# The reciprocal root of the heads' norms: three Newton steps on VectorE for one power on GpSimd

## The chip, the cores and the metric

One core of one Trainium2 chip runs the whole program. The metric is device time in microseconds (us), from the program's start to its end. In the profile, PE is TensorE (matmuls), PEld its weight loads, DVE VectorE, ACT ScalarE, POOL GpSimd and SP SyncE, which issues most transfers.

## The reference, cut to what matters

Eight batches of 256 rows by 128 features go through four layers. Each layer is attention with 16 heads of 8 features, added to `x` through a gate, and then a feed-forward part, added in the same way. The four attentions differ a little (the third, number 2, is causal), and so do the feed-forward parts. The change bears on the fourth attention alone, number 3. It scores each query by its mean cosine with all keys, and only the best fifth of the queries attend:

```python
def _L3_xattn_ref(queries, keys, values, Wq, bq, Wk, bk, Wv, bv, Wo, bo):
    ...
    q_norm = q / jnp.linalg.norm(q, axis=-1, keepdims=True)
    k_norm = k / jnp.linalg.norm(k, axis=-1, keepdims=True)
    scores_all = jnp.einsum('bhqd,bhkd->bhqk', q_norm, k_norm)
    mean_scores = scores_all.mean(axis=-1)
    u = max(1, L_q // TOP_FACTOR)
    _, top_idx = jax.lax.top_k(mean_scores, u)
    ...
```

So for each batch the reciprocal norms of 256 x 16 keys and of as many queries are needed: one array of 128 partitions by 32 numbers (2 row tiles x 16 heads) for the keys and one for the queries.

## The kernel before, in words

Each of the eight batches is a stream of steps (`stream_steps`), and up to four streams are under way at once, in four slots of buffers. One list, `SCHEDULE`, merges the streams into a single fixed order; it comes from a string of digits written out by hand (`TURNS_TAKEN`), one digit for the batch whose next step is taken. Every engine walks the same list and issues its own instructions of each step in that order, so each engine's order is fixed, and an instruction that waits holds back all that stand behind it on its engine. Eight PSUM banks are shared by all steps; the order in which they are taken is a second string of digits (`BANKS_TAKEN`). PE fills a bank only when the one who last read it has said so.

The engines speak through counting semaphores. `signals` tells how often each step raises which one, and a `Ledger` works out from it the value to wait for. Within DVE, an instruction that reads what an earlier one wrote waits for that one's end: `end(...)` raises `dve_step`, `wait_end(...)` waits for it.

The steps that matter here:

- `key_rows` (3 parts, for the keys, while layer 2 ends) and `query_rows` (5 parts, between the score tiles of layer 3) both call `rows_norms`. Part 0 adds the bias to the projected rows out of PSUM (L1169), part 1 squares them (L1174), part 2 sums the squares of each head into `ss`, 128x32 (`head_sums`, L1182). On POOL, part 2 of the same step waits for `rows_ready` and raises `ss` to the power -0.5, into `rn` (L666). It raises `rn_ready`.
- `key_unit` waits on DVE for `rn_ready` and multiplies the key rows by `rn` (L1317); PE then takes their mean (`key_mean`, L942), which ends in `kbar`.
- `query_rows` also multiplies the rows by `kbar` and sums by head into `dot` (parts 2 and 3, L1355 and L1182). Part 4 waits for `rn_ready` and multiplies `rn` by `dot` (L1363). PE turns the result (`query_means`, L965), and DVE chooses the best 51 queries of each head in 14 steps of eight at a time (`choose`, L1373 and L1375).
- `norm` has a power of its own on POOL (`rstd`, 128x2, L612) and then two instructions that norm the rows (`h`, L619). In a stream it follows `key_rows`.
- `maxima` reduces each tile of attention scores, two banks at a time, on DVE (`mx`, L1389). PE writes the tiles (L872), and once more the other way round for the attention itself (`attend`, L894), whose exponentials are ACT's (L759).
- The feed-forward part of layer 2 holds PE longest: nine experts with two runs of matmuls each (`hidden`, L1075, and `output`, L1084), of which DVE adds the results (L1261).

Of the kernel before, what the change touches and what calls it, by code (L numbers as in the profile page):

```python
# [7 lines left out]
U32 = mybir.dt.uint32  # L8
ALU = mybir.AluOpType
# [3 lines left out]
P = 128  # L13
BATCHES, ROWS, D = 8, 256, 128
HEADS, HD = 16, 8
LAYERS = 4
SLOTS = 4
RT = ROWS // P
# [36 lines left out]
TWO_ONES = 0x3F803F80  # L55
MAGIC = 1.5 * 2.0 ** 20
EXPONENT = 0x7F800000


R_BV, R_BO, R_BQ3, R_BK3, R_BF3, R_GB = 0, 4 * D, 8 * D, 9 * D, 10 * D, 11 * D  # L60
# [108 lines left out]
def signals(step, b, l, part):  # L169

    s = b % SLOTS
    return {
        "load_x": {},
        "setup": {},
        "load_weight3": {},
        "weight3": {"b_full": int((b, part) == (0, FP6_PARTS)), "b_read": int((b, part) == (0, FP6_PARTS))},
        "load_ctx": {},
        "keys": {"a_full": 1, "a_read": 1, "b_full": 1, "b_read": 1, f"hi_ready{s}": 1, f"k_split{s}": 2, f"k_moved{s}": 16 * TERMS},
        "key_rows": {"a_full": int(part == 0), "a_read": int(part == 0), "rows_ready": int(part == 2), "rn_ready": int(part == 2)},
        "key_unit": {"rows_ready": 1},  # L180
        "key_mean": {"a_full": 1, "a_read": 1},
        "stats": {"var_ready": part},
        "norm": {f"h_ready{s}": 1, "rstd_ready": int(l == 0 and b < SLOTS), "xb_ready": int(l == 2 * LAYERS - 1)},
        "turn": {"b_full": 1, "b_read": 1},
        "query": {"b_full": 1, "b_read": 1, f"hi_ready{s}": 1, f"q_split{s}": 2, f"q_moved{s}": 16 * TERMS},
        "query_rows": {"a_full": int(part == 0), "a_read": int(part == 0), "rows_ready": int(part in (2, 4)), "rn_ready": int(part == 2)},
        "query_means": {"b_full": 1, "b_read": 1},
        "choose": {"sel_ready": int(part == 2 * ROUNDS - 1)},
        "chosen": {"a_full": 1, "a_read": 1},
        "maxima": {"a_full": 2, "a_read": 1},  # L190
        "max_parts": {"m_parts_done": part, "xb_ready": int(part == 0)},
        "max_turn": {"b_full": 1, "b_read": 1, f"m_moved{s}": 16},
        "attend": {"b_full": 2, "b_read": 2, "causal_ready": int(l == CAUSAL)},
        "weigh": {"pv_done": 1, "c_read": int(part % 4 == 3)},
        "max_clear": {f"m_cleared{s}": 16},
        "heads": {"a_full": RT, "a_read": 1},
        "heads_turn": {"b_full": 1, "b_read": 1},
        "project": {"a_full": 1, "a_read": 1},
        "route0": {name: int(part == 0) for name in ("a_full", "a_read", "b_full", "b_read")},
        "gelu0": {"cubic_ready": int(part == 1), "tanh_ready": int(part == 1)},  # L200
        "blend0": {"x_done": int(part == 2)},
        "logits": {"a_full": int(part == 0), "a_read": int(part == 0), "gap_ready": int(part == 2), "gap_exp": int(part == 2)},
        "combine": {"comb_ready": int(part == COMBINED)},
        "comb_turn": {"b_full": 1, "b_read": 1},
        "out_bias": {"a_full": RT, "a_read": RT},
        "hidden": ({"a_full": 2, "a_read": 2, "tanh_ready": 2} if l == 1 else {"b_full": 2, "b_read": 2}),
        "output": ({} if (l, part) == (1, EXPERTS) else {"b_full": 1, "b_read": 1, f"out_added{s}": 1} if l == 1
                   else {"a_full": 1, "a_read": 1}),
        "quantise": {"fp6_scaled": int(part == 2), "fp6_divided": int(part == 3),
                     "fp6_rounded": int(part == FP6_PARTS - 2), "xd_ready": int(part == FP6_PARTS - 1)},  # L210
        "affine3": {"a_full": RT, "a_read": RT},
        "store": {},
    }[step]
# [114 lines left out]
def flamingo(nc, x, ctxT, attn_w, bias_cols, bias_rows, g_all, router0, block0, router1, fc1, fc2,  # L328
             gate_up, down, router2, w1, ws1, b1_cols, w2, ws2, b2_all, w3, ident_in, causal_qk,
             causal_kq, before_in, iota_in, out):  # L330
    with ExitStack() as ctx:
# [3 lines left out]
        def two(name, shape, dt=F32):  # L335

            return [sb(f"{name}{s}", shape, dt) for s in range(SLOTS)]
# [36 lines left out]
        mhalf = sb("mhalf", [P, RT * HEADS])  # L374
# [28 lines left out]
        ss = two("ss", [P, RT * HEADS])  # L403
        rn = two("rn", [P, RT * HEADS])
        dot = two("dot", [P, RT * HEADS])
        kbar = two("kbar", [P, D])
        work = two("work", [HEADS, SENT + ROWS])
        top8q = two("top8q", [HEADS, 8])
# [10 lines left out]
        work_rows = [[t[:, i, :].rearrange("p (t d) -> p t d", t=RT) for t in raw] for i in range(4)]  # L419
# [13 lines left out]
        sems = {name: sem(name) for name in SEMAPHORES}  # L433
# [154 lines left out]
        def _(pool):  # L588
# [6 lines left out]
            w = Walk()  # L595
            for w.i, (step, b, l, part) in enumerate(SCHEDULE):
                s = b % SLOTS
                if step in ("keys", "query"):

                    name, parts = ("k", k_parts) if step == "keys" else ("q", q_parts)  # L600
# [8 lines left out]
                if step == "norm":  # L609
# [5 lines left out]
                    else:  # L615
                        power.then_inc(sems["pool_step"], 1)
                        pool.wait_ge(sems["pool_step"], w.step())
                        for r in range(RT):
                            ins = nc.gpsimd.tensor_scalar(h[s][:, r, :], (x_in if l == 0 else xs)[s][:, r, :], mv[s][:, r, 0:1],  # L619
                                                          rstd[s][:, r:r + 1], ALU.subtract, ALU.mult)  # L620
# [15 lines left out]
                if step == "output" and l == 1 and part != EXPERTS:  # L636

                    n = min(part, EXPERTS)
# [13 lines left out]
                if step == "quantise" and part in (3, FP6_PARTS - 1):  # L652
# [6 lines left out]
                    else:  # L659
                        pool.wait_ge(sems["fp6_rounded"], w.at_step("fp6_rounded", 1, "quantise", b, l, FP6_PARTS - 2))  # L660
                        nc.gpsimd.tensor_tensor(blocks(h[s][:, :, :]), blocks(y), per_block(sc3[s][:, :], RT), ALU.mult)\
                            .then_inc(sems["xd_ready"], 1)
                if step in ("key_rows", "query_rows") and part == 2:

                    pool.wait_ge(sems["rows_ready"], w.at("rows_ready", 1))
                    nc.gpsimd.tensor_tensor(rn[s][:, :], ss[s][:, :], mhalf[:, :], ALU.pow)\  # L666
                        .then_inc(sems["rn_ready"], 1)


        @block.scalar  # L670
# [426 lines left out]
        def _(dve):  # L1097
# [43 lines left out]
            w = Walk()  # L1141
# [9 lines left out]
            def end(ins, *what):  # L1151

                ins.then_inc(sems["dve_step"], 1)
                ended[what] = w.step()

            def wait_end(*what):

                dve.wait_ge(sems["dve_step"], ended[what])
# [6 lines left out]
            def rows_norms(part, name, s, bias):  # L1165

                if part == 0:
                    dve.wait_ge(sems["a_full"], w.at("a_full", 1))
                    nc.vector.tensor_tensor(work_rows[0][s][:, :, :],  # L1169
                                            a_bank(w, 1)[:, 0:RT * D].rearrange("p (t d) -> p t d", t=RT),  # L1170
                                            bias, ALU.add).then_inc(sems["a_read"], 1)
                if part == 1:
                    dve.wait_ge(sems["a_read"], w.at_step("a_read", 1, name, b, l, 0))
                    end(nc.vector.tensor_tensor(work_rows[1][s][:, :, :], work_rows[0][s][:, :, :],  # L1174
                                                work_rows[0][s][:, :, :], ALU.mult), name, "squares", b)
                if part == 2:
                    wait_end(name, "squares", b)
                    head_sums(ss[s], work_rows[1][s]).then_inc(sems["rows_ready"], 1)

            def head_sums(dst, src):  # L1180

                return nc.vector.tensor_reduce(dst[:, :].rearrange("p (c h) -> p c h", h=PAIRS),  # L1182
                                               src[:, :, :].rearrange("p t d -> p (t d)")
                                               .rearrange("p (c d h) -> p c h d", d=HD, h=PAIRS), AX.X, ALU.add)
# [103 lines left out]
            for w.i, (step, b, l, part) in enumerate(SCHEDULE):  # L1288
                s = b % SLOTS
                if step == "setup" and b == 0 and part != 2:  # L1290
                    set_up(part)
                if step == "weight3" and b == 0 and part < FP6_PARTS:
# [4 lines left out]
                    ins = fp6(part, 0, 1, w3_sb.unsqueeze(1), work_rows[0][0][:, 0:1, :])  # L1297
# [24 lines left out]
                if step == "stats" and part == 0:  # L1322
# [4 lines left out]
                    for r in range(RT):  # L1327
                        ins = nc.vector.bn_stats(stats[s][:, r, :], (x_in if l == 0 else xs)[s][:, r, :])
# [12 lines left out]
                if step == "norm" and l == 0 and b < SLOTS:  # L1341

                    dve.wait_ge(sems["rstd_ready"], w.at("rstd_ready", 1))
                    for r in range(RT):
                        ins = nc.vector.tensor_scalar(h[s][:, r, :], x_in[s][:, r, :], mv[s][:, r, 0:1],
                                                      rstd[s][:, r:r + 1], ALU.subtract, ALU.mult)
# [38 lines left out]
                if step == "maxima":  # L1385
                    r, keys, hp0, n = MAX_TILES[l][part]
# [42 lines left out]
                if step == "affine3":  # L1429
                    n = 2 * LAYERS - 1  # L1430
# [6 lines left out]
                if step == "route0" and part == 0:  # L1437
# [9 lines left out]
                    for r in range(RT):  # L1447
                        wait_end("above", b, r)
                        ins = nc.vector.scalar_tensor_tensor(junk[:, r, :], a_bank(w, 1)[:, 0:ROWS], col[s][:, 0, r:r + 1],
                                                             before[:, r, :], ALU.is_equal, ALU.mult,  # L1450
                                                             accum_out=col[s][:, 2, r:r + 1])
# [9 lines left out]
                if step == "gelu0":  # L1461
# [8 lines left out]
                    if part == 2:  # L1470
                        wait_end("kept", b)
                        for r in range(RT):
                            ins = nc.vector.tensor_scalar(h[s][:, r, :], h[s][:, r, :], col[s][:, 5, r:r + 1], None, ALU.mult)
                        end(ins, "skipped", b)
                if step == "blend0":
# [4 lines left out]
                    if part == 1:  # L1480
                        wait_end("gelu", b)
                        wait_end("skipped", b)
                        for r in range(RT):
                            ins = nc.vector.scalar_tensor_tensor(h[s][:, r, :], ffo[s][:, r, :], col[s][:, 4, r:r + 1],
                                                                 h[s][:, r, :], ALU.mult, ALU.add)
# [35 lines left out]
                if step == "quantise" and part not in (3, FP6_PARTS - 1):  # L1521
# [6 lines left out]
                    ins = fp6(part, s, RT, h[s][:, :, :], h[s][:, :, :])  # L1528
# [72 lines left out]
```

## Time and profile before

| | |
|---|---|
| time, median of three runs | 946.31 us (942.61 to 951.45) |
| time of the profiled execution | 943.03 us |
| its span, first to last instruction | 941.3 us |
| PE busy | 884.7 us (94%) |
| DVE busy | 699.1 us (74%) |
| ACT busy | 638.8 us (68%) |
| POOL busy | 497.7 us (53%) |

The span is what the profile's rows cover; the time of the execution holds some 1.7 us around it. A busy share is a mean over stages with different limits. A row of the timeline gives start, duration, engine, line, operation, operands with their shapes, and in brackets how long the engine stood idle before it and whose signal ended that. Neighbours on one engine can overlap by a little where neither waits for the other.

### The profile page before, as it was taken

The page shows a single profiled execution, that of the slowest core. Times are in us where ns is not written, and L with a number is a line of the kernel's source. Part 1 is how long each engine was busy: PE and PEld are TensorE (multiplying, and loading weights), DVE is VectorE, ACT ScalarE, POOL GpSimd, SP SyncE. Part 2 cuts the span into 40 slices and gives each one's busy share as a digit, 9 for nine tenths or more (in the row PEclk, how much of TensorE's full clock was granted, in tenths as well). Part 3 has the DMA queues.
Part 4 walks back from the last instruction along what each step waited for, and adds up shares of the span by engine and source line. Part 5 has one row for each costly group of instructions (what it writes and reads, how often), then busy time and mean ns, then how long its engine had stood idle before and what let it go on. Part 6 is the DMA issues. An engine that isn't in the chain of part 4 may idle for free.

```text
span 941.3 us, 21994 instructions
## 1 busy us (share of the span) xinstructions
PE 884.7 (94%) x8025; PEld 605.6 (64%) x8025; DVE 699.1 (74%) x2142; ACT 638.8 (68%) x1460; POOL 497.7 (53%) x627
## 2 busy tenths in 40 slices
PE   7898899999999999999987999999999999999976
PEld 3344457855899987468543365756588987878533
DVE  7898988777543278986998999797735356666897
ACT  2687667767774545798775767767797448786851
POOL 6447555875961234655366365557672625533173
PEclk9999999999999999999999999999999999999999
DMA  5433332321100010002102021111110010000000
GB/s 152 113 95 98 80 103 51 82 53 37 28 23 24 15 38 3 20 25 59 40 21 74 21 70 32 30 43 30 35 39 2 18 35 1 20 19 18 21 3 24
DMA packets 67515, 39.89 MB, mean 42 GB/s; under 512 B 8263, under 2 KB 65376, under 8 KB 67408
## 3 DMA queue, kind: packets, MB, share of 16 engines
q1 hardware_dynamic: 62608, 30.44, 12.6%
q0 software_dynamic: 2208, 6.78, 2.6%
q10 hardware_dynamic: 2592, 1.26, 0.5%
q8 instruction: 65, 1.06, 0.5%
q14 instruction: 42, 0.34, 0.1%
HBM read 11.12 MB, written 1.05 MB: 13 GB/s over the span
## 4 chain that ended last, share of the span: by engine, by line
PE 59%; DVE 19%; POOL 9%; ACT 4%; issue 3%; DMA 3%; SPq 2%; POOLq 0%; DVEq 0%; ACTq 0%
PE banks L1084 12%; PE banks L1075 12%; DVE mx L1389 9%; PE banks L1044 6%; PE banks L908 6%; POOL h L619 4%; PE banks L1054 4%; PE banks L894 4%; PE banks L859 3%; PE banks L872 3%; POOL rn L666 2%; ACT probs L759 2%; PE banks L852 2%; PE banks L1015 2%; POOL rstd L612 2%
## 5 line engine op out<-in xcount | busy, mean ns | idle before, releaser
L1389 DVE TENSOR_REDUCE mx<-banks 128x4 f32<-128x1024 f32 (+1 forms) x240 | 282.9, 1214 | 23.9 <-PE banks L872 17.1
L759 ACT ACTIVATE probs<-banks 128x512 f32<-128x512 f32 (+1 forms) x512 | 258.7, 583 | 47.3 <-PE banks L894 44.8
L812 ACT ACTIVATE probs<-banks,b_sb 128x256 f32<-128x256 f32 x288 | 118.0, 474 | 73.1 <-PE banks L1075 71.5
L908 PE MATMUL banks<-probs,v_aug 128*9 128x256 f32 (+1 forms) x2048 | 146.9, 369 | 6.4 <-ACT probs L759 5.4
L1084 PE MATMUL banks<-w_sb,probs 128*128 128x128 f32 x1152 | 140.6, 277 | 0.2 <-ACT probs L759 0.2
L1084 PEld LDWEIGHTS banks<-w_sb,probs 128*128 128x128 f32 x1152 | 134.9, 192 | 5.6 <-issue 2.5
L1075 PE MATMUL banks<-hT,w_sb 128*128 128x256 f32 x576 | 137.4, 382 | 0.1
L612 POOL TENSOR_TENSOR rstd<-veps,mhalf 128x2 f32<-128x2 f32 x64 | 46.2, 723 | 159.6 <-DVE veps L1336 159.3
L666 POOL TENSOR_TENSOR rn<-ss,mhalf 128x32 f32<-128x32 f32 x16 | 88.0, 5501 | 52.0 <-DVE ss L1182 51.6
L1075 PEld LDWEIGHTS banks<-hT,w_sb 128*128 128x128 f32 x576 | 104.5, 190 | 14.7 <-DVE xs L1261 0.8
L1261 DVE SCALAR_TENSOR_TENSOR xs<-banks,comb,xs 128x128 f32<-128x128 f32 x144 | 43.6, 343 | 86.6 <-PE banks L1084 86.4
L894 PE MATMUL banks<-q_st,k_st 64*128 64x256 bf16 (+1 forms) x1024 | 93.2, 268 | 4.9 <-DMA q_st<-mT 3.3
L872 PE MATMUL banks<-k_st,q_st 64*128 64x256 bf16 (+1 forms) x1024 | 88.9, 267 | 9.0 <-DVE mx L1389 4.8
L619 POOL TENSOR_SCALAR h<-xs,mv,rstd 128x128 f32<-128x128 f32 x112 | 90.8, 817 | 5.9
L644 POOL TENSOR_TENSOR xs<-xs,raw 128x256 f32<-128x256 f32 x72 | 52.8, 734 | 48.7 <-ACT raw L800 46.6
L894 PEld LDWEIGHTS banks<-q_st,k_st 64*128 64x128 bf16 x1024 | 34.5, 94 | 68.0 <-issue 23.0
L1044 PE MATMUL banks<-hT,fc_sb 128*128 128x256 f32 x320 | 77.0, 384 | 0.0
L690 ACT ACTIVATE hT<-banks 128x256 f32<-128x256 f32 x96 | 37.0, 390 | 58.1 <-PE banks L852 57.7
L908 PEld LDWEIGHTS banks<-probs,v_aug 128*9 128x9 f32 x2048 | 34.2, 88 | 60.7 <-ACT probs L759 24.7
L872 PEld LDWEIGHTS banks<-k_st,q_st 64*128 64x128 bf16 x1024 | 36.8, 94 | 55.3 <-issue 19.5
L650 POOL TENSOR_SCALAR_AFFINE_SELECT probs<-probs 128x512 f32<-128x512 f32 x64 | 40.6, 644 | 53.4 <-ACT probs L759 53.2
L1044 PEld LDWEIGHTS banks<-hT,fc_sb 128*128 128x128 f32 x320 | 57.8, 190 | 8.2 <-issue 0.6
(197 smaller groups left out, 1463.8 us busy)
## 6 DMA issues: line engine op xcount, KB each, us to landing
k_st<-k_parts SPq DMA_DIRECT2D x192, 64.0 KB, 2.1
q_st<-q_parts SPq DMA_DIRECT2D x186, 64.0 KB, 2.1
w_sb<-in_w POOLq DMA_DIRECT2D x16, 256.0 KB, 3.6
fc_sb<-in_fc POOLq DMA_DIRECT2D x6, 256.0 KB, 4.2
x_in<-in_x SPq DMA_DIRECT2D x8, 128.0 KB, 4.0
cT<-in_ctxT SPq DMA_DIRECT2D x8, 128.0 KB, 2.7
out_x<-xs SPq DMA_DIRECT2D x8, 128.0 KB, 1.9
q_st<-mT SPq DMA_DIRECT2D x32, 16.0 KB
```

The source lines that it names most:

```text
L612: power = nc.gpsimd.tensor_tensor(rstd[s][:, :], veps[s][:, :], mhalf[:, 0:RT], ALU.pow)
L619: ins = nc.gpsimd.tensor_scalar(h[s][:, r, :], (x_in if l == 0 else xs)[s][:, r, :], mv[s][:, r, 0:1], rstd[s][:, r:r + 1], ALU.subtract, ...
L666: nc.gpsimd.tensor_tensor(rn[s][:, :], ss[s][:, :], mhalf[:, :], ALU.pow)\
L759: nc.scalar.activation(probs[s][:, part % UNIT_RING, 2 * a:2 * a + 2, 0:n], b_bank(w, a + 1)[:, 0:2 * n].rearrange("p (j q) -> p j q", j=2 ...
L812: ins = nc.scalar.activation(hid[s][:, part % UNIT_RING, c, :], b_bank(w, half + 1)[:, j * ROWS:(j + 1) * ROWS], ACT.Gelu, bias=b1_sb[:, p ...
L872: ins = nc.tensor.matmul(a_bank(w, a + 1)[:, i * keys:(i + 1) * keys], head_rows(q_st, s, a, hp0 + i, r * P, P), head_rows(k_st, s, a, hp0 ...
L894: ins = nc.tensor.matmul(b_bank(w, a + 1)[:, j * n:(j + 1) * n], head_rows(k_st, s, a, 2 * g + j, t * P, P), head_rows(q_st, s, a, 2 * g + ...
L908: ins = nc.tensor.matmul(c_bank(b, l, u // 4)[VW * i:VW * i + VR, g % 2, q0:ROWS], v_aug[s][:, t, 4 * g + i, :], probs[s][:, u % UNIT_RING ...
L1044: ins = nc.tensor.matmul(a_bank(w, k + 1)[:, a * ROWS:(a + 1) * ROWS], fc1_sb[:, 2 * part + k, a, :], hT[s][:, :], start=True, stop=True)
L1075: ins = nc.tensor.matmul(b_bank(w, half + 1)[:, j * ROWS:(j + 1) * ROWS], w1_sb[:, part, 2 * half + j, :], hT[s][:, :], start=True, stop=True)
L1084: ins = nc.tensor.matmul(a_bank(w, 1)[:, r * D:(r + 1) * D], hid[s][:, part % UNIT_RING, c, r * P:(r + 1) * P], w2_sb[:, part, c, :], star ...
L1389: nc.vector.tensor_reduce(mx[s][:, r, :, hp0:hp0 + n], banks[:, first:first + 2, :].rearrange("p a (n k) -> p a n k", n=n), AX.X, ALU.max) ...
```

## The change

The head sums stay on DVE, and the power goes. DVE works out `rn` itself, right behind `ss`: a first guess from the number's bits (read as an integer, halved, and taken from a constant), and then three Newton steps for the reciprocal root, of three instructions each. Each of the ten waits for the one before. The last raises `rn_ready`, as POOL's power did. `rows_ready` is raised once less in each step, since no other engine reads `ss`. A new buffer `halves` holds what the Newton steps need. The order of the steps and the banks stays.

```diff
+ROOT_SEED = 1597463007.0
+ROOT_ROUNDS = 3
...
-        "key_rows": {"a_full": int(part == 0), "a_read": int(part == 0), "rows_ready": int(part == 2), "rn_ready": int(part == 2)},
+        "key_rows": {"a_full": int(part == 0), "a_read": int(part == 0), "rn_ready": int(part == 2)},
...
-        "query_rows": {"a_full": int(part == 0), "a_read": int(part == 0), "rows_ready": int(part in (2, 4)), "rn_ready": int(part == 2)},
+        "query_rows": {"a_full": int(part == 0), "a_read": int(part == 0), "rows_ready": int(part == 4), "rn_ready": int(part == 2)},
...
+        halves = two("halves", [P, RT * HEADS])
...
-                if step in ("key_rows", "query_rows") and part == 2:
-
-                    pool.wait_ge(sems["rows_ready"], w.at("rows_ready", 1))
-                    nc.gpsimd.tensor_tensor(rn[s][:, :], ss[s][:, :], mhalf[:, :], ALU.pow)\
-                        .then_inc(sems["rn_ready"], 1)
...
                 if part == 2:
                     wait_end(name, "squares", b)
-                    head_sums(ss[s], work_rows[1][s]).then_inc(sems["rows_ready"], 1)
+                    end(head_sums(ss[s], work_rows[1][s]), name, "sums", b)
+                    wait_end(name, "sums", b)
+                    end(nc.vector.tensor_scalar(rn[s][:, :].bitcast(U32), ss[s][:, :].bitcast(U32), -0.5, ROOT_SEED, ALU.mult, ALU.add), name, "root", b)
+                    for n in range(ROOT_ROUNDS):
+                        wait_end(name, "root", b)
+                        end(nc.vector.tensor_tensor(halves[s][:, :], rn[s][:, :], rn[s][:, :], ALU.mult), name, "root", b)
+                        wait_end(name, "root", b)
+                        end(nc.vector.scalar_tensor_tensor(halves[s][:, :], halves[s][:, :], -0.5, ss[s][:, :], ALU.mult, ALU.mult), name, "root", b)
+                        wait_end(name, "root", b)
+                        ins = nc.vector.scalar_tensor_tensor(rn[s][:, :], halves[s][:, :], 1.5, rn[s][:, :], ALU.add, ALU.mult)
+                        if n + 1 < ROOT_ROUNDS:
+                            end(ins, name, "root", b)
+                    ins.then_inc(sems["rn_ready"], 1)
```

## Rows read from the trace of the kernel before

**Rows 1.** The page, busy us, share of the span and instructions.

```profile
PE 884.7 (94%) x8025; PEld 605.6 (64%) x8025; DVE 699.1 (74%) x2142; ACT 638.8 (68%) x1460; POOL 497.7 (53%) x627
```

**Rows 2.** The page, chain that ended last, share of the span by line.

```profile
PE banks L1084 12%; PE banks L1075 12%; DVE mx L1389 9%; PE banks L1044 6%; PE banks L908 6%; POOL h L619 4%; PE banks L1054 4%; PE banks L894 4%; PE banks L859 3%; PE banks L872 3%; POOL rn L666 2%; ACT probs L759 2%; PE banks L852 2%; PE banks L1015 2%; POOL rstd L612 2%
```

**Rows 3.** That chain in order of time, its powers: start us, us, what.

```profile
396.66 5.43 POOL rn L666
...
813.27 5.45 POOL rn L666
...
821.07 5.43 POOL rn L666
...
863.21 5.59 POOL rn L666
```

**Rows 4.** Line 666: duration ns min/median/max, first and last start; who waited.

```profile
L666 POOL TENSOR_TENSOR rn<-ss,mhalf x16: 5426/5460/5579, 241.5 to 896.5; 128x32 f32<-128x32 f32 x16
...
  DVE raw L1317: 3.4, 3
  DVE rn L1363: 2.1, 2
```

**Rows 5.** Stretches: length, busy us (count) of PE, PEld, DVE, ACT, POOL; clock; DMA.

```profile
241.00:277.00 36.00, 36.00 (x278) 31.66 (x277) 20.71 (x95) 27.32 (x64) 31.12 (x25) 1.00 0.13 33
348.00:372.00 24.00, 24.00 (x206) 19.92 (x204) 20.60 (x38) 11.35 (x26) 13.06 (x6) 1.00 0.07 16
390.00:403.00 13.00, 11.14 (x118) 6.04 (x117) 12.83 (x45) 8.16 (x18) 11.81 (x4) 1.00 0.03 7
474.00:481.00 7.00, 7.00 (x78) 3.74 (x80) 6.90 (x21) 5.73 (x13) 6.26 (x2) 1.00 0.00 0
668.00:690.00 22.00, 22.00 (x258) 14.62 (x255) 14.77 (x49) 19.76 (x39) 18.56 (x15) 1.00 0.09 22
731.00:738.00 7.00, 7.00 (x51) 6.55 (x50) 1.68 (x7) 3.35 (x9) 6.68 (x3) 1.00 0.00 0
...
813.00:827.00 14.00, 14.00 (x120) 11.45 (x120) 11.17 (x30) 12.84 (x24) 13.63 (x6) 1.00 0.03 7
863.00:870.00 7.00, 7.00 (x65) 5.88 (x62) 5.23 (x11) 5.67 (x10) 6.27 (x2) 1.00 0.01 2
896.00:903.00 7.00, 5.83 (x50) 2.83 (x49) 6.83 (x21) 1.42 (x3) 6.47 (x3) 1.00 0.01 2
```

**Rows 6.** Timeline, two powers on POOL, and DVE beside them.

```profile
390.99 11.10 POOL L666 TENSOR_TENSOR rn<-ss,mhalf 128x32 f32<-128x32 f32 x2 [2.36 <-DVE ss L1182]
...
395.53 0.40 DVE L1174 TENSOR_TENSOR raw<-raw 128x256 f32<-128x256 f32 x1
...
398.58 0.18 DVE L1363 TENSOR_TENSOR rn<-rn,dot 128x32 f32<-128x32 f32 x1
...
401.24 0.17 DVE L1336 TENSOR_SCALAR veps<-mv 128x2 f32<-128x2 f32 x1
```

**Rows 7.** Timeline, PE where that piece of the chain ends.

```profile
411.46 0.61 PE L894 MATMUL banks<-q_st,k_st 64*128 64x256 bf16 x8 [0.68 <-DMA q_st<-mT]
```

**Rows 8.** Timeline, DVE: three dependent small instructions, and a scalar_tensor_tensor.

```profile
383.29 0.19 DVE L1402 SCALAR_TENSOR_TENSOR m_parts<-mx,m_parts 128x32 bf16<-128x32 f32 x1
...
790.34 0.18 DVE L1239 TENSOR_TENSOR hot<-iota,topf 128x32 f32<-128x32 f32 x1
790.55 0.19 DVE L1246 TENSOR_TENSOR hot<-hot,col 128x32 f32<-128x32 f32 x1
790.78 0.18 DVE L1251 TENSOR_TENSOR comb<-hot 128x16 f32<-128x16 f32 x1
```

**Rows 9.** Timeline, a product on DVE beside an addition on POOL.

```profile
902.07 0.72 POOL L633 TENSOR_TENSOR xs<-xs,gbo 128x256 f32<-128x256 f32 x1
...
902.20 0.64 DVE L1363 TENSOR_TENSOR rn<-rn,dot 128x32 f32<-128x32 f32 x1
```

**Rows 10.** Line 1389, the tile maxima: who waited for it, us, times.

```profile
  PEld banks L872: 14.2, 29
```

## The prediction

> **What bounds the kernel now.** I read the busy shares first, then the chain of work that ended last, then busy time by stretches, then what each engine does around the instructions that change. PE is busy for 884.7 of 941.3 us and DVE for 699.1; POOL, which loses work here, only for 497.7 [rows 1]. So the first question is whether POOL's power is ever what PE waits for. The chain says so for 2% of the span [rows 2]: four of the sixteen powers lie on it, 5.43 + 5.45 + 5.43 + 5.59 = 21.9 us [rows 3]. That is what came last at each link, though, and not what PE would gain, for PE takes its work in one fixed order and is mostly full. The sixteen powers take 5.46 us each and start from 241.5 to 896.5; DVE waited for them five times, 3.4 + 2.1 = 5.5 us in all [rows 4]. In the stretches that hold them PE is busy without a break in most: 36.00 of 36, 24.00 of 24, 22.00 of 22, 7.00 of 7, 14.00 of 14. It has holes at 390 to 403 (11.14 of 13) and at 896 to 903 (5.83 of 7), and there it is DVE that is full: 12.83 of 13, 6.83 of 7. At 474 to 481 DVE is full as well, 6.90 of 7 [rows 5]. That is where the kernel hangs on DVE, and DVE is the engine that gets the new work.
>
> **What goes.** Sixteen powers on POOL, 16 x 5.46 = 87 us of POOL time. Two things could be late next. The first is what stands behind a power in POOL's order. Behind the pair at 390.99 to 402.09 it is the rstd of a norm, whose input DVE finished at 401.24 + 0.17 = 401.41 [rows 6]; so it comes forward by at most 0.68 us, and PE's hole at the end of that piece of chain is 0.68 us too [rows 7]. At the chain's other three powers (813, 821, 863) PE is full (14.00 of 14, 7.00 of 7), and what POOL does earlier there meets a PE that can't take it. The second is DVE's own waits for the power, 5.5 us, which go whole, but in stretches where PE is full. Together I count -2 us, between 0 and -6.2 (5.5 + 0.7).
>
> **What comes.** Ten instructions on DVE for each power, 128x32 each: the guess, and three times three. Each waits for the end of the one before, so they don't overlap. Three dependent instructions, two of this shape and a third of 128x16, stand in the trace: 0.18 to 0.19 us long, started 0.21 and 0.23 us apart [rows 8]. A scalar_tensor_tensor of this shape takes 0.19 as well [rows 8]. So 10 x 0.23 = 2.3 us; the guess (one input, one scalar pair) may be a little shorter, and the first wait on the head sums adds as much. Sixteen chains hold DVE for 37 us and add about 16 x 10 x 0.185 = 30 us to its busy time. The trace of before has no Newton chain, so the bounds: 10 x 0.185 = 1.9 us with no gap, and, if one of the nine two-input instructions meets a POOL instruction, 0.45 us more for each meeting (a 128x32 product at 902.20 took 0.64 and not 0.18, and it ended 0.05 us after POOL's addition of 902.07 to 902.79 [rows 9]). I take 2.3, the row of the dependent three.
>
> The ten stand in DVE's order at one place, so all that follows on DVE is later by 2.3 us: the tile maxima of other batches, whose PSUM banks PE needs again (PE's loads waited 29 times for them, 14.2 us in all [rows 10]), and the batch's own later steps. Whether PE feels it differs by place [rows 5]:
>
> Four powers lie where DVE has no idle time: two at 390 to 403, one at 474, one at 896. DVE's idle is 0.17, 0.10 and 0.17 us there. Nothing covers: 4 x 2.3 = 9.2 us.
>
> Five lie where PE is full but DVE nearly so: two at 348 to 372 (DVE idle 3.4 of 24), the first of two at 668 to 690, one at 787, one at 863 (idle 1.8 of 7; the one at 787 is like it and not shown). The cover is some 1.7 us of DVE idle beside each; what is left is 2.3 - 1.7 = about 0.5 each, 2.5 us. Bounds: 0, if PE's banks are far enough ahead, and 2.3 each, 11.5, if they are not.
>
> Seven lie where DVE is lighter: three at 241 to 277 (idle 15.3 of 36), the second of the two at 668 to 690, one at 732 (idle 5.3 of 7), and the two at 813 to 827 (idle 2.8 of 14), where DVE now waits for the power anyway. PE's long feed-forward runs cover them: 0. If that cover were gone it would be 7 x 2.3 = 16 us; PE at 7.00 of 7 beside a DVE at 1.68 says it isn't.
>
> **The sum.** 9.2 + 2.5 + 0 - 2 = +9.7 us, on the profiled execution's 943.0: 952.7. That execution lies 3.3 us under the median of the three runs (946.3), so the time I forecast for the median is 956.0, 1.0% slower. The bounds of the parts make -6.2 + 9.2 = +3 at the low end and 9.2 + 11.5 = +21 at the high end.
>
> **A rule weighed.** While the power ran, 390.99 to 402.09, DVE's square of two SBUF operands at 395.53 took 0.40 and its 128x32 product at 398.58 took 0.18, as long as anywhere [rows 6]; an addition on POOL did hold a product back [rows 9]. The Trainium skill (SBUF — State Buffer, section SBUF: two separate sides) says that a GpSimd instruction that reads SBUF and a DVE instruction with two SBUF inputs exclude each other for the whole of whichever starts first. By that rule the power would hold such DVE work back for up to 5.4 us and its removal would free DVE; the trace contradicts it for the power and agrees for the short addition.
>
> **The rivals.**
>
> Faster, by POOL's queue: the four powers on the chain are what the end hangs on. At those places 21.9 us go and 4 x 2.3 = 9.2 come: -12.7, 930 on the profiled execution, 934 for the median. For it: the chain names them. Against: PE is full at three of the four, and at the fourth only 0.68 us can be had. It decides from the point where PE would have been idle for the power's length, which no row of PE shows.
>
> Faster, by a lock: the power holds up DVE's two-input work, 5.46 - 2.3 = 3.2 us gained at each of the four dense places, -12.6, also 934. Rows 6 speak against it. This is what the rule of the Trainium skill above (SBUF — State Buffer) would make of it.
>
> No change: DVE's delay never reaches PE except in the dense places, and there part of it falls into holes that PE has anyway for other reasons (1.9 us at 390 to 403, 1.2 at 896) and into the removed waits: 9.2 - 3.1 - 5.5 = about +1, 947. For it: DVE is idle for a quarter of the span. Against: those holes are DVE's own making, and move with it.
>
> Slower still: the chains meet POOL's work, which now runs where the powers stood. Two meetings of 0.45 a chain make it 3.2 us: 4 x 3.2 + 5 x 1.4 - 2 = +18, 964. For it: rows 9. Against: next to the dense powers POOL has little else to do (at 390 to 403 all but 0.8 of its 11.81 us is the two powers).
>
> That the powers don't go, or the chain is shorter than ten, can't be: the code has them one by one.
>
> **How the numbers follow.** My forecast 0.45 (its own range 951 to 962), no change 0.27, slower still 0.17, POOL's queue 0.08, the lock 0.03. The range is 944 to 967: it holds the first three, from 3 us under the no-change case (the three runs lay 943 to 951) to 946.3 + 21, and leaves out the two faster ones, 0.11, and a little at the top. About 1% is what a measurement of this kernel can tell from no change, that is 937 to 956. Faster by more: 0.10, the two faster cases less a little. The forecast stands on the upper bound, so its 0.45 splits, 0.28 above and 0.17 below; with 0.17 of the slower case that makes 0.45 slower, and 0.45 the same.
>
> **What would show it.** Right: POOL busy near 410 us, DVE near 729; ten rows per chain, 0.17 to 0.20 us each, about 0.23 apart; the maxima after a chain late, and PE's holes near 390 to 403, 474 and 896 larger, by about 9 us in all; PE still full at 241 to 370 and 684 to 760. Wrong: PE's holes unchanged (then the delay was covered), a chain of over 3 us (then POOL's work was met), or PE's busy time ending earlier than now by the chain's four powers.

## The result, and the profile after

The changed kernel takes 975.62 us, the median of four runs (973.22 to 977.69), against 945.10 for the kernel before (942.61 to 951.45, four runs). The ratio on record is 1.030, with a 95% interval of 1.0269 to 1.0331 (the plain quotient of the two medians is 1.032; such ratios can differ by 0.002). That is 3% slower, where 1% was forecast and 967 was the top of the range. The profiled execution took 976.67 us, with a span of 974.6, that is 33.3 us more than before.

The page of the changed kernel, busy us by engine, then the granted TensorE clock in 40 slices:

```profile
PE 898.9 (92%) x8025; PEld 611.0 (63%) x8025; DVE 732.8 (75%) x2302; ACT 638.4 (66%) x1460; POOL 410.1 (42%) x611
...
PEclk9998999999999999999999999999999999999988
```

Against [rows 1], POOL has lost 87.6 us and DVE has gained 33.7, about as forecast (410 and 729). PE runs the same 8025 matmuls, and they hold it 14.2 us longer. Its idle time (span less busy) went from 941.3 - 884.7 = 56.6 to 974.6 - 898.9 = 75.7, by 19.1. These two make the 33.3.

One chain in DVE's timeline, the first of the two dense ones at 390 to 403 in [rows 5]'s time, with what follows on DVE:

```profile
400.75 0.59 DVE L1192 TENSOR_REDUCE ss<-raw 128x32 f32<-128x256 f32 x1
401.38 0.18 DVE L1178 TENSOR_SCALAR rn<-ss 128x32 uint32<-128x32 uint32 x1
401.59 0.19 DVE L1181 TENSOR_TENSOR halves<-rn 128x32 f32<-128x32 f32 x1
401.82 0.19 DVE L1183 SCALAR_TENSOR_TENSOR halves<-halves,ss 128x32 f32<-128x32 f32 x1
...
403.40 0.19 DVE L1185 SCALAR_TENSOR_TENSOR rn<-halves,rn 128x32 f32<-128x32 f32 x1
403.51 0.42 DVE L1365 TENSOR_TENSOR raw<-raw,kbar 128x256 f32<-128x256 f32 x1
...
404.73 0.42 DVE L1427 TENSOR_TENSOR resid<-banks,rden 128x256 f32<-128x256 f32 x1
```

Each of the ten takes 0.18 to 0.19 us and starts 0.21 to 0.23 after the one before, as the three of [rows 8] did. The chain is 403.40 + 0.19 - 401.38 = 2.21 us long. Behind it in DVE's order stands, among others, the `resid` of another batch. PE's timeline of the changed kernel shows who waited for that (in brackets PE's idle time ahead of the row, and what ended it):

```profile
357.93 0.92 PE L1073 MATMUL banks<-hT,w_sb 128*128 128x256 f32 x3 [1.18 <-DVE mx L1399]
...
405.21 0.44 PE L850 MATMUL banks<-ident,resid 128*128 128x128 f32 x2 [2.65 <-DVE resid L1427]
...
492.53 0.69 PE L850 MATMUL banks<-ident,resid 128*128 128x128 f32 x2 [2.21 <-DVE resid L1427]
...
693.09 0.39 PE L870 MATMUL banks<-k_st,q_st 64*128 64x256 bf16 x4 [2.62 <-DVE mx L1399]
...
894.30 0.91 PE L1073 MATMUL banks<-hT,w_sb 128*128 128x256 f32 x3 [1.36 <-DVE mx L1399]
...
929.02 0.70 PE L844 MATMUL banks<-zeros 128*128 128x512 bf16 x2 [3.30 <-DVE mx L1399]
```

The first of the two rows on `resid` has this counterpart in the kernel before, with a hole of 0.41 us; the hole has grown by 2.24, one chain:

```profile
392.53 0.44 PE L852 MATMUL banks<-ident,resid 128*128 128x128 f32 x2 [0.41 <-DVE resid L1417]
```

The others are waits for the tile maxima. The answer to [rows 10], now of L1399, says the same in sum: 14.2 us, 29 times, has become

```profile
  PEld banks L870: 20.2, 37
```

The stretches of [rows 5], each from the same matmul to the same matmul in the changed kernel (785 to 792, the power at 787, is one more than there). The columns are those of [rows 5]:

```profile
244.96:282.31 37.35, 36.04 (x278) 31.66 (x277) 25.77 (x123) 27.30 (x64) 14.88 (x22) 1.00 0.13 32
353.30:382.44 29.14, 24.86 (x206) 19.66 (x204) 25.34 (x57) 11.33 (x26) 2.57 (x4) 1.00 0.06 14
400.44:417.93 17.49, 12.65 (x118) 6.89 (x117) 16.64 (x65) 8.15 (x18) 1.40 (x2) 0.90 0.02 5
488.23:498.92 10.69, 8.48 (x78) 4.29 (x80) 9.05 (x31) 5.79 (x13) 1.32 (x2) 0.84 0.00 0
688.08:714.63 26.55, 23.63 (x258) 15.03 (x255) 20.28 (x69) 20.03 (x40) 8.33 (x13) 0.94 0.07 18
755.63:762.63 7.00, 7.00 (x51) 6.55 (x49) 5.34 (x30) 3.34 (x9) 1.43 (x3) 1.00 0.00 0
809.62:817.88 8.26, 6.97 (x66) 5.62 (x67) 7.28 (x29) 5.98 (x13) 3.58 (x6) 1.00 0.01 2
838.88:854.25 15.37, 14.31 (x120) 11.21 (x120) 14.51 (x53) 13.52 (x24) 4.71 (x7) 1.00 0.06 14
890.07:898.72 8.65, 7.29 (x65) 5.87 (x62) 8.14 (x25) 5.76 (x10) 0.00 (x0) 1.00 0.01 2
924.48:935.15 10.67, 7.37 (x51) 3.76 (x49) 9.56 (x32) 1.43 (x3) 0.00 (x0) 0.84 0.01 2
```

Take the second: the same 206 matmuls took 24.00 us with PE busy in all of it, and take 29.14 now, with PE busy for 24.86. A PE without a break was no cover for two chains of DVE. The sixth shows real cover: 7.00 and 7.00 of 7, though DVE went from 1.68 to 5.34. The ten stretches grew by 27.2 us in all. Of the other 6.1, 4.0 came ahead of the first chain, and 2.4 where the kernel before is at 513 to 530 and no chain stands (the last section); so much of the 33.3 between these two profiled executions does not come from waiting for a chain.

### The profile page after: what moved, and what is told of

Its sections match the earlier page's. It is cut to its first block, busy times and chain, and to the rows that moved or that the text cites. A ratio compares the mean times of both kernels' runs of the same rounds, so it can differ in the third digit from the quotient of the medians.

```text
span 974.6 us, 22138 instructions
## 1 busy us (share of the span) xinstructions
PE 898.9 (92%) x8025; PEld 611.0 (63%) x8025; DVE 732.8 (75%) x2302; ACT 638.4 (66%) x1460; POOL 410.1 (42%) x611
## 4 chain that ended last, share of the span: by engine, by line
PE 61%; DVE 21%; POOL 5%; ACT 4%; issue 3%; DMA 3%; SPq 2%; POOLq 0%; DVEq 0%; ACTq 0%
PE banks L1082 12%; PE banks L1073 11%; DVE mx L1399 9%; PE banks L906 7%; PE banks L1042 6%; PE banks L892 4%; PE banks L857 4%; PE banks L1052 4%; PE banks L870 3%; POOL h L622 3%; PE banks L1013 2%; ACT probs L757 2%; PE banks L850 2%; DMA q_st<-mT 2%; SPq L513 2%
## 5 line engine op out<-in xcount | busy, mean ns | idle before, releaser
L1399 DVE TENSOR_REDUCE mx<-banks 128x4 f32<-128x1024 f32 (+1 forms) x240 | 283.3, 1214 | 27.7 <-PE banks L870 20.7
L906 PE MATMUL banks<-probs,v_aug 128*9 128x256 f32 (+1 forms) x2048 | 150.0, 375 | 6.6 <-ACT probs L757 5.8
L892 PEld LDWEIGHTS banks<-q_st,k_st 64*128 64x128 bf16 x1024 | 34.5, 95 | 75.9 <-issue 26.1
L1512 DVE SCALAR_TENSOR_TENSOR probs<-probs,banks 128x256 f32<-128x256 f32 x80 | 32.0, 418 | 33.2 <-ACT probs L786 33.2
```

The source lines that it names most:

```text
L892: ins = nc.tensor.matmul(b_bank(w, a + 1)[:, j * n:(j + 1) * n], head_rows(k_st, s, a, 2 * g + j, t * P, P), head_rows(q_st, s, a, 2 * g + ...
L906: ins = nc.tensor.matmul(c_bank(b, l, u // 4)[VW * i:VW * i + VR, g % 2, q0:ROWS], v_aug[s][:, t, 4 * g + i, :], probs[s][:, u % UNIT_RING ...
L1399: nc.vector.tensor_reduce(mx[s][:, r, :, hp0:hp0 + n], banks[:, first:first + 2, :].rearrange("p a (n k) -> p a n k", n=n), AX.X, ALU.max) ...
```

## The experiments

Theory A, after the result: ten dependent instructions in one piece stand in DVE's fixed order; the maxima and residuals behind them come later, PE's fixed order waits for them, and PE's own busy share says nothing of how soon it runs dry. The rivals B to D are named in the expectations. All times below are medians, and each ratio is to runs of the kernel before on the same chip (medians 946.46, 945.10 and 946.63 in the three sets: the first four runs, the next three, the last three). A loss in us that stands with a ratio is the ratio's share of that median.

**The power alone.**

```diff
-ROOT_ROUNDS = 3
+ROOT_ROUNDS = 0
...
-                    end(nc.vector.tensor_scalar(rn[s][:, :].bitcast(U32), ss[s][:, :].bitcast(U32), -0.5, ROOT_SEED, ALU.mult, ALU.add), name, "root", b)
+                    ins = nc.vector.tensor_scalar(rn[s][:, :].bitcast(U32), ss[s][:, :].bitcast(U32), -0.5, ROOT_SEED, ALU.mult, ALU.add)
```

> The three Newton steps are left out: DVE runs the guess alone, one instruction of 0.2 us, and POOL has no power; the norms are rough, so other queries are chosen, as many as before. Theory A (the ten instructions stand in DVE's fixed order and hold up what PE waits for): chain 0.2 us and not 2.2, so 943 to 950, about the kernel before. Rival B (the missing power lets POOL run ahead and meet DVE, or the new buffer's place in memory costs): 965 or more, as with the change.

Measured: 947.08 us, ratio 1.0003 (0.9984 to 1.0022). Its page:

```profile
PE 887.8 (94%) x8025; PEld 607.7 (64%) x8025; DVE 703.1 (75%) x2158; ACT 638.2 (68%) x1460; POOL 410.3 (43%) x611
```

All of POOL's 87 us have gone, and nothing came of it: within the interval, some 2 us either way, the power was hidden wholly, although the chain of waits had four of them on it [rows 3].

**The chain alone**, with the power kept; `roots` is read by nobody.

```diff
+        roots = two("roots", [P, RT * HEADS])
...
                     head_sums(ss[s], work_rows[1][s]).then_inc(sems["rows_ready"], 1)
+                    dve.wait_ge(sems["rows_ready"], w.at("rows_ready", 1))
+                    end(nc.vector.tensor_scalar(roots[s][:, :].bitcast(U32), ss[s][:, :].bitcast(U32), -0.5, ROOT_SEED, ALU.mult, ALU.add), name, "root", b)
+                    for n in range(ROOT_ROUNDS):
...
```

> The kernel before with its powers on POOL, and the ten DVE instructions added at the same place, writing two buffers that nobody reads. Theory A: as slow as the change, 968 to 980, with POOL busy near 498 us again. Rival B: near the kernel before, 943 to 950.

Measured: 971.69 us, ratio 1.0258 (1.0230 to 1.0287). The chains by themselves make nearly all of the loss.

**The chain in ten pieces.** The same ten instructions, each issued behind the DVE work of a following step instead of all at once; what is left over is issued ahead of the first reader of `rn`.

```diff
+                for n, make in enumerate(chain):
+                    later.append((name, b, n, len(chain), make))
...
+                if later and (step, part) not in (("key_rows", 2), ("query_rows", 2)):
+                    one_later()
```

> The same ten instructions, but one behind each following step of the schedule and no longer in one piece (what is left is run before the first use). Theory A: no maxima wait for more than about 0.25 us, and the gaps of the chain are filled by other work: 948 to 960. Rival C (DVE's 30 us of added work count, wherever they stand): 970 or more.

Measured: 957.05 us, ratio 1.0106 (1.0071 to 1.0140). The same instructions cost about a third when they stand in pieces. The trace shows one to three of the ten in a row mostly, and five at most (1.14 us), so the expected wait of a single piece was not reached everywhere. It is the cheapest form with all sixteen chains that was run, and still slower than the power.

**Twice the steps.**

```diff
-ROOT_ROUNDS = 3
+ROOT_ROUNDS = 6
```

> Six Newton steps and not three: 19 instructions, a chain of 4.3 us and not 2.2. Theory A: each of some twelve places passes on 2.1 us more, +25, and PE's longer holes bring a few more low-clock stretches: 998 to 1012. Rival B: no more than the added busy time of DVE where it is full, four places, +8: about 984.

Measured: 1014.42 us, ratio 1.0708 (1.0682 to 1.0734), 2 us over the expected band. From 0 to 3 rounds the time rose by 975.6 - 947.1 = 28.5 us, while the sixteen chains grew in the traces from 3.4 to 38.6 us in all, by 35.2. From 3 to 6 it rose by 38.8, and the chains by 34.5, to 73.1. What cover there is goes to the first instructions; the later ones cost more than their own length. The mean granted clock was lower as well (0.959, against 0.977 in the changed kernel), and PE was busy for 913.1 us and not 898.9; how much of the excess that makes was not separated.

**Keys alone, queries alone.** One of the two steps keeps its power (the other's end has a semaphore of its own).

```diff
+ON_DVE = "key_rows"
...
+                if step in ("key_rows", "query_rows") and step != ON_DVE and part == 2:
...
+                    if name == ON_DVE:
```

> Guess and Newton steps on DVE for the keys' eight norms only; the queries' eight stay a power on POOL. Theory A, by where the start of each matmul fell behind the kernel before (2.1 us at the first keys, 2.2 at the fourth, 2.7 and its aftermath 1.8 at the fifth, nothing at the other five): +9, 950 to 958. Rival D (every chain costs the same): +15, about 960.

> The other way round: the queries' eight on DVE, the keys' eight on POOL. Theory A: +17 to +21 (3.1, 2.0, 2.3, 2.4 and its aftermath 2.7, 1.4, 1.5, 1.2, 3.4 and more in the last 40 us): 961 to 968. Rival D: +15, about 960, the same as for the keys.

Measured: keys 953.22 us, 1.0076 (1.0052 to 1.0099); queries 965.44, 1.0212 (1.0195 to 1.0229). Both lie where theory A had them, and rival D's 960 fits neither. Together they make 2.9%, the change's 3.0. Eight chains each, and the queries' cost nearly three times as much: the price hangs on the place.

**Work for PE in the holes.** Stretches of low granted clock follow some of the new holes. Matmuls on zeros were added ahead of two of them.

```diff
+    ("heads_turn", 3, 2, 0): 11, ("heads_turn", 4, 0, 0): 9}
```

> The changed kernel with 11 and 9 idle matmuls on zeros ahead of two transposes where PE stood still for 2.65 and 2.21 us with a free bank at hand (the head outputs of batch 3 in layer 2 and of batch 4 in layer 0); nothing else is changed. Theory A with a clock part (a long hole lets the granted clock fall to its low level, 1.2 GHz, for a while, and PE then works at half speed): the low stretches near 407 and 492 us are gone, and 2 to 4 us with them, 972 to 974. Without a clock part: no change, 975 to 976.

Measured: 978.05 us, 1.0333 (1.0294 to 1.0372). That is above what either case expected, though the interval reaches down to both. It is no gain, and it settles nothing. PE's timeline of this run, the added zeros and the next hole:

```profile
405.15 2.55 PE L845 MATMUL banks<-zeros 128*128 128x512 bf16 x11 [1.93 <-DVE selm L1394]
...
414.78 0.60 PE L871 MATMUL banks<-k_st,q_st 64*128 64x256 bf16 x4 [3.11 <-DVE resid L1428]
```

The bank at hand was not free: the zeros waited for the `selm` that reads it, came only after a hole of 1.93 us, and another of 3.11 followed.

**The prediction's three groups, one at a time.** As the run with the power kept, but with the chain only where `CHAINS` names it: the four dense places, the five half covered, the seven light.

```diff
+CHAINS = (("query_rows", 2), ("key_rows", 3), ("query_rows", 3), ("query_rows", 7))
...
+                    if (name, b) in CHAINS:
```

> The powers stay on POOL, and only the four chains of the places that the prediction called dense (queries of batches 2, 3 and 7, keys of batch 3) are added on DVE, into buffers that nobody reads: 4 x 2.2 = 9 us of DVE work. The prediction's term: all of it is paid, +9 us, ratio 1.010. Theory A (each chain passes on what PE has no spare time for, and more where a new hole of PE is followed by a stretch of low granted clock): the start of the same matmul moved by 4.5, 2.4 and 3.3 us over these places in the changed kernel, 10.2 in all, and two of the stretches of low clock lie behind them: +10 to +14, ratio 1.011 to 1.015. If only the meetings with POOL counted: under +3, ratio below 1.003.

> As the run before, but with the five chains of the places that the prediction called half covered (queries of batches 0, 1, 4 and 6, keys of batch 4): 11 us of DVE work. The prediction's term: 0.5 each, +2.5 us, ratio 1.003, with bounds of 0 and 11.5. Theory A: DVE's idle time beside a chain is no cover, and neither is a busy PE; the same matmul moved by 5.1, 4.5, 1.4 and 1.2 us over these places, 12.2 in all: +9 to +13, ratio 1.010 to 1.014.

> As the two runs before, but with the seven chains of the places that the prediction called light (keys of batches 0, 1, 2, 5, 6 and 7, queries of batch 5): 15.4 us of DVE work. The prediction's term: PE's long runs cover them, 0, ratio 1.000; 16 us if the cover were gone. Theory A: the same matmul moved by 2.1 and 1.5 us over these places in the changed kernel and by nothing over the others, about +4: +2 to +7, ratio 1.002 to 1.007. The three groups together should make the 2.6% of the run with all sixteen chains beside the powers; if they make much less, the chains make each other dearer.

Measured: dense 959.85 us, 1.0133 (1.0111 to 1.0154), that is 12.6 us; half covered 955.49, 1.0078 (1.0050 to 1.0107), 7.4 us; light 948.89, 1.0015 (1.0001 to 1.0030), 1.4 us. The dense run lies where theory A had it; the half covered one came out under the expected 9 to 13 us, and the light one under 2 to 7. Sum 2.26%, against 2.58% for all sixteen: the intervals overlap, so the groups may simply add up.

How many us each stretch of [rows 5] grew, from the same matmul to the same matmul, worked out from the profiled executions:

| stretch before | chains | dense run | half run | light run | changed kernel |
|---|---|---|---|---|---|
| 241 to 277 | 3 light | 0.0 | 0.0 | 1.3 | 1.4 |
| 348 to 372 | 2 half | 0.0 | 4.2 | 0.0 | 5.1 |
| 390 to 403 | 2 dense | 6.6 | 0.0 | 0.0 | 4.5 |
| 474 to 481 | 1 dense | 3.7 | 0.0 | 0.0 | 3.7 |
| 668 to 690 | 1 half, 1 light | 0.2 | 2.7 | 0.0 | 4.6 |
| 731 to 738 | 1 light | 0.0 | 0.0 | 0.0 | 0.0 |
| 785 to 792 | 1 half | 0.0 | 1.3 | 0.0 | 1.3 |
| 813 to 827 | 2 light | 0.0 | 0.0 | 1.5 | 1.4 |
| 863 to 870 | 1 half | 0.0 | 1.7 | 0.0 | 1.7 |
| 896 to 903 | 1 dense | 3.3 | 0.0 | 0.0 | 3.7 |

Among these stretches each run grows where it has chains, and by at most 0.2 us in any other, so the loss is local. The columns sum to 13.8, 9.9 and 2.8 us, 26.5 together, against 27.2 in the changed kernel: place by place, little is missing. Outside the stretches the profiled executions differ too, without a chain: by -0.7 to 4.0 us from the kernel before ahead of 241, and by up to 2.4 at 513 to 530.

The half run's waits, in PE's timeline:

```profile
354.93 0.39 PE L877 MATMUL banks<-k_st,q_st 64*128 64x256 bf16 x4 [0.52 <-DVE mx L1404]
...
372.65 0.40 PE L899 MATMUL banks<-q_st,k_st 64*128 64x256 bf16 x4 [1.84 <-DVE xs L1276]
...
680.18 0.39 PE L877 MATMUL banks<-k_st,q_st 64*128 64x256 bf16 x4 [2.15 <-DVE mx L1404]
```

In the dense run the two chains at 390 to 403 show what a dense place can cost beyond its chains. The stretch there, and the same one in the run with the power kept and all sixteen chains:

```profile
393.96:413.58 19.62, 13.89 (x118) 7.30 (x117) 18.05 (x70) 8.27 (x18) 13.52 (x5) 0.83 0.02 5
...
398.64:416.14 17.50, 11.14 (x118) 6.04 (x117) 16.65 (x65) 8.15 (x18) 12.30 (x4) 1.00 0.02 5
```

Before, it was 13.00 us with PE busy for 11.14 at a clock of 1.00 [rows 5]. In the dense run PE's idle time grew from 1.86 to 5.73, by 3.9, the two chains nearly whole; and the same 118 matmuls took 2.75 us more, at a mean clock of 0.83. In the other run the clock stayed at 1.00, and the stretch grew by 4.5, the two chains (4.4) and no more. So the low clock is not bound to the chains. Nor does it always cost time: the changed kernel grew by 4.5 here too, at 0.90, for its second hole was 1.5 us shorter than in the run with the power kept (1.61 and 3.13), and the longer matmuls filled the difference. At 474 and at 896 the dense run's clock was 0.84 and 0.83, and one chain of 2.2 us cost 3.7 and 3.3; in the changed kernel (0.84 both) it cost 3.7 each.

## Why the prediction was wrong

The direction was right, and so was the mechanism (what stands behind a chain in DVE's order is late, and PE waits for it); the size was a third of what came. The step that failed most is the cover that the prediction counted for the five half covered chains; the dense term was too small as well. Step by step:

**The chain's length, 2.3 us**, held: 2.21 to 2.22 where nothing interfered, in eleven of the sixteen. DVE's and POOL's busy times came about as forecast.

**Dense, 9.2 us**, was right in its mechanism (all of it is paid) and too small: 12.6 in its own run (interval 10.5 to 14.6), and 13.6 in the three stretches of its profiled execution. The four chains are 8.9 of that. The term had no line for matmuls that run slower behind the new holes; the other 4.7 us stand in stretches with a clock of 0.83 to 0.84.

**Half covered, 0.5 each, 2.5 in all**, is the step that failed most: 7.4 in its own run (interval 4.7 to 10.1), and 9.9 in its profiled execution, that is 1.3 to 2.7 a chain. The cover that I counted, 1.7 us of DVE's idle time beside each chain, is a sum over a stretch. An instruction behind the chain can use only the idle time that lies between the chain and itself; and PE, full as it was, waited for the first maxima or the first `xs` after it (354.93, 680.18, 372.65). My upper bound, 2.3 each, was the truer price. One of the prediction's signs failed with this term, that PE would still be full at 241 to 370: the row at 357.93 above has a hole of 1.18 us there.

**Light, 0**, was nearly right: 1.4 in its own run, 2.8 in its profiled execution. At 731 to 738 it held to the hundredth. At 241 to 277 three chains cost 1.3 us. At 813 to 827 I took DVE's waits for the power as cover as well, and 1.5 us were lost.

**What goes, -2 us**, was nothing to speak of: 1.0003. DVE's 5.5 us of waits for the power lay where PE had work, as the text said itself before it counted them.

With the measured terms the sum is 12.6 + 7.4 + 1.4 + 0 = 21.4 us, just the upper bound that the prediction gave. The change cost 3.0% of 946.3, 28.4. Of the other 7 us, 3 lie between the three groups and all sixteen together (24.4), 4 between those and the change; both are within the intervals, and the stretches, 26.5 us in the three groups and 27.2 in the changed kernel, show hardly such a gap. Part of the 4 can be read: in the changed kernel the chain at 352.90 is 3.50 us long, in the run with the power kept 2.58, and the one near 688 is 2.94 against 2.46. DVE's timeline of the changed kernel there, and POOL's:

```profile
352.90 0.19 DVE L1178 TENSOR_SCALAR rn<-ss 128x32 uint32<-128x32 uint32 x1
...
353.36 0.55 DVE L1183 SCALAR_TENSOR_TENSOR halves<-halves,ss 128x32 f32<-128x32 f32 x1
353.94 0.65 DVE L1185 SCALAR_TENSOR_TENSOR rn<-halves,rn 128x32 f32<-128x32 f32 x1
354.62 0.65 DVE L1181 TENSOR_TENSOR halves<-rn 128x32 f32<-128x32 f32 x1
355.31 0.19 DVE L1183 SCALAR_TENSOR_TENSOR halves<-halves,ss 128x32 f32<-128x32 f32 x1
```

```profile
353.14 0.71 POOL L610 TENSOR_TENSOR q_parts<-resid,q_parts 128x256 bf16<-128x256 f32 x1
353.82 1.40 POOL L636 TENSOR_TENSOR xs<-xs,gbo 128x256 f32<-128x256 f32 x2
```

Three of the ten met POOL's additions, which now run where the power stood, and took 0.55 to 0.65 us instead of 0.19. The stretches of these two chains grew by 0.9 and 0.8 us more than in the run with the power kept.

**The rivals.** POOL's queue is refuted by the first run: without the power, and with no chain in its place, the time is the same. The lock is refuted by the same run: had the power held DVE up, its removal would have shown. No change fell with the result. In the trace of before, too, the two-input instructions of DVE that ran wholly within a power took their usual time (0.40 and 0.18 us in [rows 6]). Slower still came nearest in time (964), for a reason that was a small part of it: five of the sixteen chains were longer than 2.22 us, in all by 38.6 - 16 x 2.22 = 3.1 us. The rival had 0.9 more for each chain in the nine dense and half covered places; none of the five lies in a dense place, and two in half covered ones (3.50 and 2.94 us).

**The clock's share** is not shown by a run of its own: the one that was to take it away, with zeros, did not. PE's busy time grew by 14.2 us for the same matmuls, but by 3.1 in the first run too, where no time was lost, and at 390 to 403 longer matmuls cost the changed kernel nothing. An estimate from the rows: what the two other dense places, at a clock of 0.84, cost beyond one chain each, 2 x 1.5 = 3 us of the 28.4.

## What to carry to other kernels

On an engine with a fixed order, price a chain of small dependent instructions at its whole length for whoever waits behind it, unless a row shows the idle time between the chain and the first instruction that another engine needs. Neither a busy share of that other engine, be it 100%, nor idle time somewhere in the stretch is that row. Work on an idle engine (here 87 us of powers) can be free even where the chain of waits names it, and moving it to the engine that the others wait for was then a loss in every form that was run; in pieces it was a third of the loss.

## What the runs showed of the hardware

Low granted clock also came where no chain stands. Stretches of the changed kernel near 530, same columns as above:

```profile
530.00:533.00 3.00, 1.69 (x24) 0.36 (x20) 3.00 (x3) 0.00 (x0) 1.25 (x3) 1.00 0.38 95
...
537.00:540.00 3.00, 3.00 (x16) 2.06 (x14) 1.69 (x5) 0.38 (x1) 0.00 (x0) 0.50 0.00 0
```

PE had been busy for 1.69 of 3 us at the full clock, 2.4 GHz; a little later it was busy without a break at 0.50, 1.2 GHz. In the kernel before the same place (513 to 530, PE busy for 14.50 of 17) had a mean clock of 1.00. In profile against profile the place took 2.4 us longer in the changed kernel, 2.1 in the half run and in the keys run, 0.9 in the dense run, and nothing in the run with the power kept, which came there 17 us late. So a delay earlier in the program doesn't bring the fall by itself; what does wasn't tried.

A 5.46 us power on POOL did nothing to DVE's two-input instructions (0.40 and 0.18 us within it, [rows 6]), and additions of 0.7 us on POOL stretched them from 0.19 to as much as 0.65. The Trainium skill (SBUF — State Buffer, section SBUF: two separate sides) has one rule for both, a mutual exclusion for as long as the instruction runs; the trace agrees for the additions and contradicts it for the power.
